# A masked mixing product, VectorE cycles with four tiles, and a first tile by column halves, in an fp8 and 4-bit feed-forward kernel

## The chip, the cores and the metric

The kernel runs on 1 core of one Trainium2 chip. The metric is the device time of one execution in microseconds, the median of several runs. The kernel before takes 527.69 us (three runs, 527.61 to 528.54). The traces are of one profiled execution each; its span begins with the first and ends with the last instruction.

## What is computed

x is 64 samples x 64 channels x 1024, float32. Cut to what matters:

```python
# 1: a mixture of K = 8 channel-mixing matrices, weighted per sample
att = softmax(mlp(cond))                                   # (64, 8), three layers, exact gelu
m   = einsum('boi,bih->boh', einsum('bk,koi->boi', att, weight), x) + (att @ bias_k)[:, :, None]
# 2: a linear layer in fp8 (e4m3), with ONE scale for all of m and one for the weight
xs, ws = max|m| / 448, max|W0| / 448
x1  = x + fp8(m / xs) @ fp8(W0.T / ws) * (xs * ws) + b0
# 3: a grouped convolution along the 1024 positions (64 channels, 4 groups, 9 taps) plus a per-sample
#    term, then a linear layer with 4-bit weights (groups of 128, a scale and a zero for each)
y   = conv(x1) + (c @ c_weight.T)[:, :, None] + side
out = x1 + y @ ((W1_q - zero) * scale).T + b1
```

The scale in step 2 needs the largest |m| of all 64 samples. So no tile can be quantised before every tile has been mixed and reduced.

## The kernel before

**Tiles.** Two samples of 64 channels make a tile of 128 partitions x 1024; there are T = 32. All mixed tiles stay in the buffer Y (`slot(t)`, 32 slots of 128 x 1024). Slots also hold other things until a tile is loaded there: slots 16 to 20 the 4-bit weight's row blocks 0 to 4 (`w1i(n)`), slot 21 and 22 the taps, slot 23 the small network, slots 24 to 31 the eight row slices of W0 (`w0f`).

**The opening** (lines 446 to 563, 744 to 794, 1016 to 1058). TensorE runs the three-layer network. The mixing weights, 8 x 64 x 64, are split on VectorE into three bf16 parts (`wk_parts`), and nine DMAs gather the parts into `wkp9`. The attention weights get the same split and are transposed; 32 products give the mixing matrices, which ACT and VectorE (`place_last`) copy into `mixw`, a block-diagonal 128 x 128 matrix for each tile. VectorE also takes the largest |W0| of each slice as it lands (`largest_w0`, L758). The maximum of all 128 partitions is found by a transpose and a product with ones on TensorE (`w_pe`): the exchange. Then comes the weight's scale (`scales`).

**The cycles** (lines 840 to 850). Then VectorE runs eight cycles, r = 0 to 7: round slice r of W0 to the fp8 grid (L730, L733, L735), subtract the zeros of block r of W1 (`less_w1`, L820), and reduce mixed tiles (`largest_mixed`, L805: tiles 3r+1 and 3r+2 in one instruction, then 3r+3). `groups` lists these as (first tile, tiles); an entry waits until ACT has kept its last tile. What is left of the tiles follows behind cycle 7. POOL ends the rounding (`round_w0`, L490) and multiplies W1 with its scales (`times_w1`, L484).

**TensorE and ACT** walk the tiles in order, t = 0 to 31. TensorE mixes tile t in two halves (`mixed_tile`, L1064); behind tile 3r+6 it turns slice r of W0 (`turned0`, waits for POOL's rounding), behind tile 3n+8 block n of W1 (`turned1`, waits for POOL's product; both L1080). ACT keeps tile t with its bias (L582), copies the turned blocks to `f0T` and `f1T` (L589), and behind tile 3r-1 scales slice r (`scale_w0`, L601), which for r >= 2 waits for POOL's rounding of slice r-2, whose buffer it uses again.

**SP's queue** issues loads in program order, each behind its wait. Tiles 16 to 20 wait for `less_w1` of the block whose slot they take, tiles 24 to 31 for POOL's rounding of the slice.

**The exchange of the mixed maximum, and the first tiles** (lines 851 to 968, 1214 to 1245). When the last reduction is done, TensorE transposes the maxima (L1220) between sums over the turned W1 (`weight_sums`, L1198). Then `scales`, and the first tiles: widen (L864, L868), mask the bits (L873), quantise (L882, L887), turn, multiply with W0 (`first_ffn0`, L1154), add the residual (`residual0`, L912), split x1 into two fp16 parts (`hi` on ACT L642, `lo` on VectorE L922), move the parts to the convolution's layout by eight DMAs per tile (`move`, L412 on SP and L533 on POOL), and convolve (`conv`, L1180). `keep_clock` and `keep_clock_wide` are products whose result is used nowhere.

**The steady part.** From tile 2 on, for every tile TensorE runs 16 products with W0, 32 with W1 and 48 for the convolution; the other engines and the queues work beside it.

Of the kernel before, what the change touches and what calls it, by code (L numbers as in the profile page):

```python
# [5 lines left out]
def adaln_ffn_kernel(nc, x, cond, fside, cw0, cb0, cw1, cb1, cw2, cb2, cwk, cbk,  # L6
# [21 lines left out]
    P = 128  # L28
# [23 lines left out]
    with ctx:  # L52
# [29 lines left out]
        def mix_src(m, par, b):  # L82

            return pair[m][par * C:(par + 1) * C, :].rearrange("p (j t b) -> p b t j", t=T, b=NB)[:, b]

        def mix_dst(m, par, b):
            o = b * C + 32 * m + par
            return mixw[b * C:(b + 1) * C, :, o:o + 31:2]
# [11 lines left out]

        def w1c(n):
# [12 lines left out]
        wkf, wkr = (work[0:K * KC, 5 * L + n * KF:5 * L + (n + 1) * KF] for n in range(2))  # L114
        wkp = work[0:K * KC, 6 * L:6 * L + 3 * KF // 2].bitcast(bf16).rearrange("p (e f) -> p e f", e=3)
        attp9 = slot(19)[0:B, 0:36].bitcast(bf16)
        attp = attp9.rearrange("p (k i e) -> p i e k", i=3, e=3)
        attr = slot(19)[0:B, 40:40 + K]
        attpT = slot(19)[0:KP, 64:64 + B // 2].bitcast(bf16)
# [12 lines left out]
        att = mlp[0:B, 840:848]  # L132
        attT = mlp[0:K, 848:912]
# [5 lines left out]
        mbk2 = f0T[0:K, R8 - 1, 0:2 * P].bitcast(fp32)  # L139
# [13 lines left out]
        o += R8 * SW  # L153
        convin = work[:, o:o + BG * SW].bitcast(fp16).rearrange("p (g s e) -> p g s e", g=BG, e=2)
# [50 lines left out]
        ld = {n: sem("ld_" + n) for n in ("emb", "mw0", "mw1", "mw2", "ctw", "mbk", "wk", "wkp", "wkl", "fcol", "zs", "b0", "b1",  # L205
# [16 lines left out]
        wk_parts = sem("wk_parts")  # L222
# [4 lines left out]
        att_parts = sem("att_parts")  # L227
        attp_mm = sem("attp_mm")
        attp_ev = sem("attp_ev")
# [62 lines left out]
        turns0 = {3 * r + 6: r for r in range(R8)}  # L292
        turns1 = {3 * n + 8: n for n in range(KT)}
        turn_order = []
        for t in range(T):
            if t in turns0:
                turn_order.append(("w0", turns0[t]))
            if t in turns1:
                turn_order.append(("w1", turns1[t]))

# [15 lines left out]
        def _(sp):  # L316
# [21 lines left out]
            load_w0(3)  # L338
            load_w0(4)
            for b in range(NB):  # L340
                sp.dma_start(mbk2[:, b * C:(b + 1) * C], cbk).then_inc(ld["mbk"], 16)
            load_w0(5)
            load_mixing(0)
# [4 lines left out]
            for n in range(7):  # L348
                for t in range(2 * n + 1, 2 * n + 3):
                    load_mixing(t)  # L350
                if n == 3:
                    sp.wait_ge(mix_mm, 2)
                load_w1(n)
# [4 lines left out]
            load_mixing(15)  # L358
            for t in range(16, 21):
# [4 lines left out]
            sp.wait_ge(taps_split, 4)  # L364
            load_mixing(21)
            load_mixing(22)
# [3 lines left out]
            for r in range(R8):  # L370
# [3 lines left out]
                load_mixing(W0_SLOT + r)  # L374

# [40 lines left out]
            sp.wait_ge(moved_sp[1], 32)  # L416
# [29 lines left out]
        def _(pool):  # L446
# [847 lines left out]
```

## Time and profile before

| | |
|---|---|
| median of 3 runs | 527.69 us |
| profiled execution | 527.88 us |
| its span | 526.1 us |
| TensorE busy | 511.2 us, 97% |
| VectorE busy | 414.4 us, 79% |
| ACT busy | 243.9 us, 46% |
| POOL busy | 59.3 us, 11% |

In the rows, PE is TensorE, PEld its weight loads, DVE is VectorE, ACT ScalarE, POOL GpSimd, SP SyncE; a q behind a name is the engine's own DMA queue. A line number is that of the kernel before. "out<-in" names the buffers: Y holds the tiles, work and fixed are scratch, pair is PSUM. Times are microseconds from the start of the span. In brackets stands the idle time ahead of an instruction and what ended it.

### The profile page before, as it was taken

The numbers are of one execution on the slowest core, as the hardware profiler recorded it, in microseconds if no ns is written. First come the engines' busy times: TensorE is split into PE (matmuls) and PEld (weight loads), VectorE is DVE, ScalarE is ACT, GpSimd is POOL, SyncE is SP. The second block draws the span as 40 slices with busy tenths as digits, with TensorE's granted clock in tenths as the row PEclk, the third lists the DMA queues.
The fourth block names the chain that finished last, engine by engine and source line by source line (L and its number), as shares of the span: only waits on it lengthen the run. The fifth ranks groups of instructions, "written<-read, shape, count | busy, mean of one in ns | idle before, by whom it ended". The sixth has DMA issues, their size and how long they took to land.

```text
span 526.1 us, 9556 instructions
## 1 busy us (share of the span) xinstructions
PE 511.2 (97%) x3528; PEld 286.0 (54%) x3528; DVE 414.4 (79%) x526; ACT 243.9 (46%) x286; POOL 59.3 (11%) x68
## 2 busy tenths in 40 slices
PE   5799999999999999999999999999999999999997
PEld 4544444355555555555555555555555555555564
DVE  6899999877887777777777777777777777777652
ACT  3479897754344444444444444444444444442310
POOL 5276666020000000000000000000000000000000
PEclk9999999999999999999999999999999999999999
DMA  7999681235675655566666565555566656565632
GB/s 225 393 386 405 222 329 42 80 82 142 185 218 182 181 181 181 181 181 181 181 181 181 181 181 181 181 181 181 182 183 182 182 183 180 183 185 186 199 122 80
DMA packets 85795, 100.61 MB, mean 191 GB/s; under 512 B 34484, under 2 KB 67318, under 8 KB 85782
## 3 DMA queue, kind: packets, MB, share of 16 engines
q1 hardware_dynamic: 84754, 99.41, 59.2%
q0 software_dynamic: 656, 0.82, 0.9%
q10 hardware_dynamic: 372, 0.20, 0.1%
q8 instruction: 8, 0.13, 0.1%
q14 instruction: 5, 0.04, 0.0%
HBM read 58.41 MB, written 32.75 MB: 173 GB/s over the span
## 4 chain that ended last, share of the span: by engine, by line
PE 81%; DVE 11%; issue 2%; DMA 2%; SPq 1%; ACT 1%; POOL 1%; DVEq 0%; ACTq 0%; POOLq 0%
PE pair L1190 41%; PE pair L1164 19%; PE pair L1180 16%; DVE stat L805 5%; DMA Y<-in_L_ffn_weight_dram 2%; PE pair L1154 1%; PE pair L1064 1%; DVE work L730 1%; DVE work L820 1%; DVE Y L820 1%; DVE work L733 1%; PE pair L1267 1%; SPq L337 1%; POOL fixed L490 1%; DVE work L742 1%
## 5 line engine op out<-in xcount | busy, mean ns | idle before, releaser
L1190 PE MATMUL pair<-f1T,work 128*128 128x512 f16 x1008 | 227.5, 379 | 0.0
L1190 PEld LDWEIGHTS pair<-f1T,work 128*128 128x128 f16 x1008 | 97.2, 98 | 111.7 <-DVE work L929 0.2
L609 ACT ACTIVATE work<-Y,consts 128x1024 bf16 (+1 forms) x29 | 33.3, 1149 | 185.7 <-DVE work L903 185.7
L922 DVE TENSOR_TENSOR work<-Y,work 128x512 f16<-128x512 f16 (+1 forms) x64 | 71.2, 1120 | 47.2 <-ACT work L642 46.3
L1164 PE MATMUL pair<-f0T,work 128*128 128x512 bf16 x464 | 104.9, 379 | 0.0
L1180 PEld LDWEIGHTS pair<-taps,work 128*128 128x128 f16 x1536 | 88.3, 98 | 8.0 <-issue 0.5
L1180 PE MATMUL pair<-taps,work 128*128 128x128 f16 x1536 | 91.0, 219 | 0.0
L642 ACT CAST work<-Y 128x512 f16 (+1 forms) x64 | 69.5, 1136 | 18.6 <-DVE Y L912 15.6
L935 DVE TENSOR_TENSOR Y<-pair,Y 128x512 f32 (+1 forms) x63 | 43.3, 687 | 41.3 <-PE pair L1190 41.3
L1164 PEld LDWEIGHTS pair<-f0T,work 128*128 128x128 bf16 x464 | 45.3, 98 | 54.8
L1064 PE MATMUL pair<-Y,work 128*128 128x512 f32 x128 | 60.6, 608 | 0.4 <-ACT Y L582 0.4
L647 ACT CAST work<-pair 128x512 f16<-128x512 f32 x64 | 37.1, 585 | 33.4 <-PE pair L1180 31.9
L941 DVE SCALAR_TENSOR_TENSOR pair<-work,consts,fixed 128x512 f32<-128x512 f32 x63 | 47.3, 753 | 0.1
L912 DVE SCALAR_TENSOR_TENSOR Y<-pair,stat,Y 128x512 f32 (+1 forms) x64 | 45.0, 743 | 1.2 <-PE pair L1164 1.2
L929 DVE TENSOR_TENSOR work<-pair,work 128x512 f16<-128x512 f32 x64 | 41.2, 683 | 2.5 <-ACT work L647 2.5
L582 ACT ACTIVATE Y<-pair,consts 128x1024 f32<-128x1024 f32 (+1 forms) x33 | 35.9, 1092 | 12.4 <-PE pair L1064 12.3
L896 DVE SCALAR_TENSOR_TENSOR Y<-work,Y 128x1024 bf16 (+1 forms) x29 | 35.5, 1225 | 4.0
L805 DVE TENSOR_REDUCE stat<-Y 128x1 f32<-128x1024 f32 (+2 forms) x23 | 36.4, 1629 | 0.7 <-ACT Y L582 0.6
L903 DVE SCALAR_TENSOR_TENSOR work<-work,Y 128x1024 bf16<-128x1024 bf16 x29 | 35.5, 1225 | 1.2
L1064 PEld LDWEIGHTS pair<-Y,work 128*128 128x128 f32 x128 | 22.8, 194 | 22.0 <-issue 20.4
L610 ACT ACTIVATE Y<-Y,stat (+1 forms) x29 | 32.9, 1134 | 0.0
L490 POOL TENSOR_TENSOR fixed<-Y,work 128x1024 bf16<-128x1024 f32 x8 | 24.0, 3004 | 18.6 <-DVE Y L735 18.6
(161 smaller groups left out, 251.5 us busy)
## 6 DMA issues: line engine op xcount, KB each, us to landing
Y<-in_x_dram SPq DMA_DIRECT2D x64, 512.0 KB, 3.9
out_dram<-Y SPq DMA_DIRECT2D x31, 512.0 KB, 3.7
split_rows<-work SPq DMA_DIRECT2D x30, 520.0 KB, 2.6
work<-split_rows SPq DMA_DIRECT2D x30, 520.0 KB, 3.9
Y<-in_L_ffn_weight_dram SPq DMA_DIRECT2D x8, 512.0 KB, 7.3
Y<-in_L_ffn_W_q_dram SPq DMA_DIRECT2D x5, 512.0 KB, 14.2
work<-in_L_ffn_W_q_dram SPq DMA_DIRECT2D x3, 512.0 KB, 15.2
work<-work SPq DMA_DIRECT2D x8, 65.0 KB, 3.7
```

The costliest lines, as they stand in the source:

```text
L642: nc.scalar.copy(split[:, r, h:h + S, 0], v[:, r, :]).then_inc(hi_done, 1)
L647: nc.scalar.copy(y1s[n][:, 0, :, b * C:(b + 1) * C].rearrange("p r (g a) -> p g r a", g=G), ps[4 + b][:, :].rearrange("p (g r a) -> p g r ...
L805: nc.vector.tensor_reduce(stat[:, n:n + 1], part, AX.X, ALU.max, apply_absolute_value=True).then_inc(mixed_red, 1)
L912: nc.vector.scalar_tensor_tensor(out=v, in0=ps[h][:, :], scalar=acc_neg, in1=v, op0=ALU.mult, op1=ALU.add).then_inc(x1_done, 1)
L922: nc.vector.tensor_tensor(split[:, r, s, 1], v[:, r, :], split[:, r, s, 0], ALU.subtract)\
L929: nc.vector.tensor_tensor(part(1), ps[4 + b][:, :].rearrange("p (g r a) -> p g r a", g=G, r=R8), part(0), ALU.subtract).then_inc(ylo_done, 1)
L935: nc.vector.tensor_tensor(v, ps[2 + h][:, :], v, ALU.add).then_inc(res_done, 1)
L941: nc.vector.scalar_tensor_tensor(out=ps[2 + h][:, :], in0=wsum[:, c], scalar=ctxcol[:, bass.ds(t, 1)], in1=fixed[:, c], op0=ALU.mult, op1= ...
L1064: last = mm(ps[2 * (t % 2) + h][:, :], mixw[:, t, :], slot(t)[:, h * H:(h + 1) * H], start=True, stop=True)
L1164: last = mm(ps[h][:, :], qT[n][:, k, :], f0T[:, k, h * H:(h + 1) * H], start=(k == 0), stop=(k == KT - 1))
L1180: last = mm(ps[4 + b][:, g * P:(g + 1) * P], convin[:, b * G + g, h:h + S, xp], taps16[:, wp, h, g].rearrange("p r a -> p (r a)"), start=( ...
L1190: last = mm(ps[2 + h][:, :], y1s[n][:, e, k, :], f1T[:, k, h * H:(h + 1) * H], start=False, stop=(e == 1 and k == KT - 1), skip_group_chec ...
```

## The change

**Mixing matrices.** The three-part split and its gathers go. `wkf` becomes 128 rows (8 matrices x 16 groups of 4 output channels) of 256; the attention weights, repeated 16 times, are transposed and multiplied with a mask `own_c` (the columns of an identity summed), which gives `attM`, 128 x 16 x 64. Four fp32 products of 512 columns give the mixing matrices. The first load of `wkf` moves from ACT's queue to POOL's.

**Order.** Two slices of W0 are reduced ahead of `place_last`, six behind it. Tiles 0 to 2 are reduced within the exchange of the weight's maximum, whose transpose stands behind tile 3 on TensorE and whose product stands within tile 4. The cycles take four tiles each (0 to 4), then three. The turns stand at other tiles, the last three behind all tiles. The last tile is loaded to scratch and is not blocked by slice 7.

**First tiles.** The first product runs by column halves, its residual, split and low part too. Ten of the idle products near the first convolution become six.

The diff, cut to its core:

```diff
-        KP = 9 * K
-        wkp9 = Y[0:KP, 20 * L:22 * L].bitcast(bf16)
-        KC = C // K
+        KC = P // K
         KF = C * C // KC
+        KR = K * KC
+        wkf = work[0:KR, 5 * L:5 * L + KF]
+        attM = work[0:KR, 6 * L:6 * L + KC * B].rearrange("p (c b) -> p c b", c=KC)
...
-        groups = [(0, 1)] + [g for r in range(R8) for g in ((3 * r + 1, 2), (3 * r + 3, 1))]
-        groups += [(25, 2), (27, 2), (29, 1), (30, 1), (31, 1)]
-        groups[-1:] = [(31, 0), (31, 1)]
+        beside = [[(0, 1), (1, 1)], [(2, 1)]]
+        cycle_groups = [[(3, 2), (5, 2)], [(7, 2), (9, 2)], [(11, 2), (13, 2)], [(15, 2), (17, 2)], [(19, 2), (21, 2)],
+                        [(23, 2), (25, 1)], [(26, 2), (28, 1)], [(29, 2), (31, 0), (31, 1)]]
...
-        turns0 = {3 * r + 6: r for r in range(R8)}
-        turns1 = {3 * n + 8: n for n in range(KT)}
+        turns0 = {3 * r + 9 if r < R8 - 1 else T - 1: r for r in range(R8)}
+        turns1 = {3 * n + 10: n for n in range(KT - 2)}
...
@@ sync
-            for e in range(2):
-                sp.wait_ge(wk_parts, (1, 3)[e])
-                for i in range(3):
-                    sp.dma_start(wkp9[3 * i + e:KP:9, :], wkp[:, e, :]).then_inc(ld["wkp"], 16)
             load_w0(3)
+            load_mixing(0)
+            sp.wait_ge(mbk_zero, 1)
...
             load_mixing(15)
+            sp.wait_ge(taps_split, 4)
+            load_mixing(21)
+            load_mixing(22)
             for t in range(16, 21):
                 sp.wait_ge(w1_less, t - 15)
                 load_mixing(t)
             sp.wait_ge(wT_mm, turn_at("w1", 1) + 1)
             load_w1(7)
-            sp.wait_ge(taps_split, 4)
-            load_mixing(21)
-            load_mixing(22)
...
-            for r in range(R8):
+            for r in range(R8 - 1):
                 sp.wait_ge(w0q, r + 1)
                 if r < 2:
                     sp.wait_ge(wT_mm, turn_at("w1", 3 + r) + 1)
                 load_mixing(W0_SLOT + r)
+            for h in range(2):
+                sp.wait_ge(w1_less, 6 + h)
+                sp.dma_start(last_raw(h), x_t[T - 1, :, h * H:(h + 1) * H]).then_inc(ld_x[T - 1], 16)
...
@@ scalar
+                    if t == T - 1:
+                        act.wait_ge(w0q, R8)
                     nc.scalar.activation(slot(t)[:, c], pair[t % 2][:, c], ACT.Identity, bias=aggcol[:, t:t + 1])\
...
-                if t == 2:
+                if t == 5:
                     act.wait_ge(w_step, 2)
-                if t % 3 == 2 and t <= 20:
-                    scale_w0(t // 3 + 1)
+                if t % 3 == 2 and 5 <= t <= 23:
+                    scale_w0(t // 3)
...
+            for n in (KT - 2, KT - 1):
+                keep_w1(n)
             keep_sums(0)
...
             first_scaled(2)
+            act.wait_ge(pads, 3)
+            first_hi(0)
             for h in range(2):
                 keep_first_q(1, h)
-            act.wait_ge(pads, 3)
-            hi(0)
+            first_hi(1)
...
@@ vector
-            for r in range(1, 5):
-                largest_w0(r)
-            place_last()
-            for r in range(5, R8):
+            largest_w0(0)
+            largest_w0(1)
...
+            place_last()
+            for r in range(2, R8):
                 largest_w0(r)
             dve.wait_ge(w_red, R8)
             nc.vector.tensor_reduce(w_part, w_rows, AX.X, ALU.max).then_inc(w_red, 1)
+            largest_mixed(0)
+            largest_mixed(1)
             dve.wait_ge(w_pe, 1)
             nc.vector.tensor_reduce(w_all, ps[7][0:1, 0:P], AX.X, ALU.max).then_inc(w_red, 1)
+            largest_mixed(2)
             dve.wait_ge(w_pe, 2)
...
                 less_w1(r)
-                if r == 0:
-                    largest_mixed(0)
-                largest_mixed(2 * r + 1)
-                largest_mixed(2 * r + 2)
-            for n in range(2 * R8 + 1, NGRP):
-                largest_mixed(n)
+                for g in cycle_groups[r]:
+                    largest_mixed(groups.index(g))
...
             first_widen(1)
-            first_quantise(1)
+            first_quantise(1, (0,))
             dve.wait_ge(x_step, 4)
-            residual0(0, 0, 16)
+            residual0(0, 0, 16, (0,))
+            first_quantise(1, (1,))
+            residual0(0, 0, 16, (1,))
+            first_lo(0)
+            first_lo(1)
             first_widen(2)
-            lo(0)
...
@@ tensor
+            pe.wait_ge(idle_zero, 1)
+            keep_clock(5, H)
...
-            for q in range(4):
-                for j in range(8):
-                    o2 = 8 * q + j
-                    last = mm(ps[q][:, j * B:(j + 1) * B], wkp9[:, o2 * 2 * C:(o2 + 1) * 2 * C],
-                              attpT, start=True, stop=True)
-                if q % 2:
-                    last.then_inc(mix_mm, 1)
+            for h in range(2):
+                pe.wait_ge(mlp_ev, 8 + h)
+                for m in range(2):
+                    last = mm(ps[2 * h + m][:, :], wkf[:, m * 2 * C:(m + 1) * 2 * C],
+                              attM[:, h * KC // 2:(h + 1) * KC // 2].rearrange("p c b -> p (c b)"),
+                              start=True, stop=True)
+                last.then_inc(mix_mm, 1)
...
-                if t == 0:
+                if t == 3:
                     pe.wait_ge(w_red, R8 + 1)
                     nc.tensor.transpose(ps[7][0:1, 0:P], w_part, ident[:, :]).then_inc(w_pe, 1)
...
-            pe.wait_ge(wT_ev, 2 * KT)
+            for n in (KT - 2, KT - 1):
+                turned1(n)
+            pe.wait_ge(wT_ev, 2 * KT - 2)
...
+            pe.wait_ge(wT_ev, 2 * KT)
             weight_sums(1, range(KT))
...
-            first_ffn0(0, 0, 0)
+            first_ffn0_by_columns()
...
-            keep_clock_wide(10)
+            keep_clock_wide(6)
```

## Rows read from the trace of the kernel before

**Rows 1.** The page: busy engines, and TensorE's clock in 40 slices.
```profile
PE 511.2 (97%) x3528; PEld 286.0 (54%) x3528; DVE 414.4 (79%) x526; ACT 243.9 (46%) x286; POOL 59.3 (11%) x68
...
PEclk9999999999999999999999999999999999999999
```

**Rows 2.** Chain that ended last: start us, us, engine, tile, line, how many.
```profile
30.18 4.45 DVE stat L805 x3
...
115.39 3.45 PE pair L1154 x16
```

**Rows 3.** A stage: window and length, busy us (how many) by engine, clock, DMA share, GB/s.
```profile
15.00:45.00 30.00, 28.61 (x140) 15.87 (x141) 27.61 (x32) 21.18 (x26) 15.97 (x12) 1.00 1.03 396
```

**Rows 4.** Timeline of cycle 1: start us, us, engine, line, operation, out<-in.
```profile
34.54 0.42 DVE L730 TENSOR_SCALAR work<-work 128x1024 int16<-128x1024 int16 x1
...
36.66 1.22 DVE L820 TENSOR_TENSOR work<-Y,small 128x1024 f16<-128x1024 int32 x1
36.83 3.05 POOL L490 TENSOR_TENSOR fixed<-Y,work 128x1024 bf16<-128x1024 f32 x1 [1.10 <-DVE Y L735]
...
37.80 3.41 DVE L805 TENSOR_REDUCE stat<-Y 128x1 f32<-128x2048 f32 x2
...
41.12 0.91 DVE L730 TENSOR_SCALAR work<-work 128x1024 int16<-128x1024 int16 x1
```

**Rows 5.** Timeline around the turn of the last slice of W0.
```profile
76.22 3.65 PE L1064 MATMUL pair<-Y,work 128*128 128x512 f32 x8
...
78.19 1.11 ACT L582 ACTIVATE Y<-pair,consts 128x1024 f32<-128x1024 f32 x1 [0.20 <-PE pair L1064]
...
79.71 0.65 PE L1080 MATMUL pair<-small,work 128*128 128x128 f16 x8
...
82.35 0.62 PE L1080 MATMUL pair<-small,fixed 128*128 128x128 bf16 x8 [0.22 <-POOL fixed L490]
...
85.93 3.41 DVE L805 TENSOR_REDUCE stat<-Y 128x1 f32<-128x2048 f32 x2
```

**Rows 6.** SP's queue: the load of tile 20, and its time to landing (line 321).
```profile
59.12 0.34 SPq L321 DMA_DIRECT2D Y<-in_x_dram  x1
...
DMA to landing us min/median/max: 3.2/3.2/3.2
```

**Rows 7.** Groups of 0 to 115 us: busy us, mean ns | idle before.
```profile
L589 ACT COPY f0T<-pair 128x1024 bf16<-128x1024 bf16 x8 | 8.1, 1012 | 0.0
...
L484 POOL TENSOR_TENSOR work<-work,small 128x1024 f16<-128x1024 f16 x5 | 9.6, 1911 | 0.0
...
L601 ACT ACTIVATE work<-Y,stat 128x1024 bf16<-128x1024 f32 x7 | 8.0, 1138 | 0.0
```

**Rows 8.** Timeline of the opening.
```profile
8.40 1.89 PE L1014 MATMUL pair<-small 128*128 128x128 bf16 x16
...
15.11 1.89 PE L1047 MATMUL pair<-Y 72*128 72x64 bf16 x32 [1.70 <-DMA Y<-work]
...
20.34 2.55 PE L1064 MATMUL pair<-Y,work 128*128 128x512 f32 x4
...
22.71 1.22 DVE L758 TENSOR_REDUCE stat<-Y 128x1 f32<-128x1024 f32 x1 [0.17 <-DMA Y<-in_L_ffn_weight_dram]
...
26.84 0.43 DVE L730 TENSOR_SCALAR work<-work 128x1024 int16<-128x1024 int16 x1
```

**Rows 9.** Timeline of the exchange of the mixed maximum.
```profile
89.91 2.41 DVE L805 TENSOR_REDUCE stat<-Y 128x1 f32<-128x1024 f32 x3 [0.56 <-ACT Y L582]
...
92.58 0.27 PE L1220 MATMUL pair<-ident,stat 128*1 128x128 f32 x1 [0.96 <-DVE stat L852]
...
94.33 0.88 DVE L864 TENSOR_SCALAR work<-Y,stat 128x512 bf16<-128x512 f32 x2
```

**Rows 10.** Timeline of the first tiles.
```profile
104.99 2.12 DVE L922 TENSOR_TENSOR work<-Y,work 128x512 f16<-128x512 f32 x2 [0.19 <-ACT work L642]
...
112.54 2.85 PE L1180 MATMUL pair<-taps,work 128*128 128x128 f16 x48
```

More of the change, by code:

```diff
@@ L107, in adaln_ffn_kernel @@
         mixw = work[:, 0:T * P].rearrange("p (t m) -> p t m", t=T)
-        KP = 9 * K
-        wkp9 = Y[0:KP, 20 * L:22 * L].bitcast(bf16)
-        KC = C // K
+        KC = P // K
         KF = C * C // KC
[L114 to L119, printed above, removed]
+        KR = K * KC
+        wkf = work[0:KR, 5 * L:5 * L + KF]
+        attM = work[0:KR, 6 * L:6 * L + KC * B].rearrange("p (c b) -> p c b", c=KC)
+        idle_rows = f1T[:, 0, 0:H]
         wide_taps = f0T[:, 0, 0:CG * R8 * 4].bitcast(fp32).rearrange("p (c j) -> p c j", c=CG)
@@ L642, in hi, with first_hi @@
                     nc.scalar.copy(split[:, r, h:h + S, 0], v[:, r, :]).then_inc(hi_done, 1)
+            def first_hi(h):
+                act.wait_ge(x1_done, h + 1)
+                s = slice(h * S // 2, (h + 1) * S // 2)
+                v = slot(0).rearrange("p (s u r) -> p u r s", u=2, r=R8 // 2)
+                nc.scalar.copy(skewed[:, :, :, s, 0], v[:, :, :, s]).then_inc(hi_done, 1)
             def yhi(t, n):
@@ L913, in residual0, with first_lo @@
                                                    op1=ALU.add).then_inc(x1_done, 1)
+            def first_lo(h):
+                dve.wait_ge(hi_done, h + 1)
+                s = slice(h * S // 2, (h + 1) * S // 2)
+                v = slot(0).rearrange("p (s u r) -> p u r s", u=2, r=R8 // 2)
+                nc.vector.tensor_tensor(skewed[:, :, :, s, 1], v[:, :, :, s], skewed[:, :, :, s, 0], ALU.subtract)\
+                    .then_inc(lo_done, 1)
             def lo(t):
@@ L1055, in _, with turned_tap_rows @@
-            last.then_inc(taps_mm, 1)
+            nc.tensor.transpose(ps[6][0:KR, 256:256 + B], attR, ident[0:B, 0:B]).then_inc(mlp_mm, 1)
+            def turned_tap_rows(ws):
+                pe.wait_ge(taps_made, 3)
+                for w in ws:
+                    last = nc.tensor.transpose(pair[2][:, w * P:(w + 1) * P],
+                                               taps_rows[:, w].rearrange("p c r -> p (c r)"), ident[:, :])
+                if w == R8 - 1:
+                    last.then_inc(taps_mm, 1)
@@ L1063, in mixed_tile @@
                 for h in range(2):
-                    last = mm(ps[2 * (t % 2) + h][:, :], mixw[:, t, :], slot(t)[:, h * H:(h + 1) * H],
-                              start=True, stop=True)
+                    raw = last_raw(h) if t == T - 1 else slot(t)[:, h * H:(h + 1) * H]
+                    last = mm(ps[2 * (t % 2) + h][:, :], mixw[:, t, :], raw, start=True, stop=True)
                     if h or t == T - 1:
                         last.then_inc(mixed, 1)
-                    if t == 1 and h == 0:
+                    if t == 4 and h == 0:
                         pe.wait_ge(w_red, R8 + 2)
@@ L1142, in keep_clock_wide, with first_ffn0_by_columns @@
                     mm(ps[5][:, :], ident_b, f0T[:, 0, 0:H], start=True, stop=True)
+            def first_ffn0_by_columns():
+                for h in range(2):
+                    pe.wait_ge(shifted_ev, h + 1)
+                    for k in range(KT):
+                        if h == 0 and k % 4 == 0:
+                            pe.wait_ge(qT_in[0], 2 * k + 8)
+                        last = mm(ps[h][:, :], qT[0][:, k, :], f0T[:, k, h * H:(h + 1) * H],
+                                  start=(k == 0), stop=(k == KT - 1))
+                    last.then_inc(f0_done, 1)
             def first_ffn0(t, n, before):
```

178 lines of the change are left out of this document (82 added, 96 removed).

## The prediction, made before the changed kernel ran

> **What bounds the kernel now.** I read the page first: a span of 526.1 us, TensorE busy 97% of it [rows 1]. Then the chain of work that ended last, which falls into two parts: up to about 92 us it runs mostly on VectorE, through the reductions that look for the largest mixed value; from 115.39 us on it is TensorE without a break [rows 2]. The change touches nothing there. So its worth is how much earlier or later that part starts. I call S the start of the first widening (line 864), which needs the scale of all mixed tiles: 94.33 us now [rows 9].
>
> **The VectorE cycles.** Before S, VectorE runs eight cycles, one for each slice r of the first weight. I call C_r the start of line 730 in cycle r; C_0 is 26.84 [rows 8]. Counted from C_r = 34.54: the rounding is done and `less_w1` starts at +2.12, ends at +3.34, the reductions start at +3.26 (starts overlap ends a little), and the next cycle starts at +6.58 [rows 4]. So a pair of tiles and a single one together take 3.32. In the first cycle two singles and a pair take 4.45 [rows 2]: a single 1.12, a pair 2.20. The last three, a single and two halves, take 2.41 [rows 9]: a half 0.66. Line 730 takes 0.42 when POOL is idle and 0.91 when POOL's product of the cycle before still runs, as in most cycles now [rows 4]. POOL rounds slice r until C_r + 5.34 (36.83 + 3.05 [rows 4]); its product of 1.91 follows [rows 7].
>
> **The change, part by part.**
>
> *Opening.* The split weights, their gather DMAs and three bf16 parts go; four fp32 products on a masked operand replace them. Now the first mixed tile starts at 20.34, 5.2 us behind the 32 products that wait for the gather until 15.11 [rows 8]. The four new products need no gather; at half a tile's time each (0.87, as two tiles take 3.49 from 76.22 to 79.71 [rows 5]) and with the same copies behind them they allow the first tile at about 17 to 18. That isn't what starts the cycles. That is the eight reductions of the weight. Two now stand ahead of `place_last` and six behind it: if it is done at 17, six times 1.15 lead to 23.9, as now (22.71 + 1.22 [rows 8]), although the last slice, whose load waits no longer for the split, should land 2 to 3 us earlier. Then come the reductions of three tiles, put into the exchange of the weight's scale (3.4 us), and the exchange itself, now 2.9 from 23.93 to 26.84 [rows 8], of which they fill about 1.0. Sum: 23.9 + 3.4 + 1.9 = 29.2 for C_0, 2.4 later, with three tiles done. The exchange stands behind tiles 3 and 4 on TensorE, whose loads arrive at 396 GB/s, 1.3 us each [rows 3]; that leaves C_0 between 28 and 30.5.
>
> *Work in the cycles.* Cycles 0 to 4 reduce four tiles: 3.26 + 2 x 2.20 = 7.66, and POOL is through (5.34 + 1.91 = 7.25, with its issue 7.4) just before the next line 730, so that this is taken at 0.42. Cycles 5 and 6: 6.58 each. Cycle 7: 3.26 + 2.20 + 1.32 = 6.78. Sum 58.2. With no wait VectorE would be through at 29.2 + 58.2 = 87.4, against 92.32 now [rows 9].
>
> *Waits in the cycles.* The turns of the weight move three tiles back (slice r behind tile 3r + 9), the loads of tiles 16 to 20 stay behind `less_w1`, and the reductions move forward: cycle r wants tiles up to 4r + 6. These cross. From rows: 1.97 after TensorE starts a tile (76.22), ACT starts to keep it (78.19) and takes 1.11, so VectorE has it 3.1 after the start; a tile behind a turn that waited for POOL until 82.3 is reduced from 85.93, 3.6 later [rows 5]. ACT takes 1.01 for a turn, 1.14 for `scale_w0` [rows 7].
> Cycle 2: ACT's own load, with turns and scales beside the tiles, gives tile 14 between 0 and 2.1 late; I take 1.0.
> Cycle 3 wants tile 18. ACT must first do `scale_w0(5)`, which waits for POOL's round 3 (+5.34); then 1.14 + 1.12 and issue: +7.7 against +5.46. **2.2**.
> Cycle 4 wants tiles 19 and 20 at +3.26, but tile 20's slot is the source of `less_w1(4)`, so its load is issued only when that ends, at +3.34. Now the same load is issued at 59.12, right behind its `less_w1`, (SP's queue had waited for it), and lands 3.2 later [rows 6], but is reduced two cycles later. Landed +6.6, free for VectorE +9.7: **6.4**. Behind it stands the load of the last W1 piece, then tiles 23 to 25; they arrive in time.
> Then tile 22: ACT has `scale_w0(6)`, tile 21, the turn of slice 4 and tile 22, 4.4 us, while VectorE has 2.20 of work: **2.2**.
> Cycle 5 wants tile 24: ACT stands at `scale_w0(7)` for round 5: +7.7 against +3.26: **4.4**. Tile 25 follows in time.
> Cycle 6 wants tile 28, which TensorE mixes behind turn 6: 5.34 + 3.6 = +9.0 against +5.46: **3.5**.
> Cycle 7: tile 31 is kept after round 7: **0.6**.
> Sum 20.3; VectorE is through at 107.7. None of these waits exists now; the one wait shown for a tile is 0.56, before the last reductions [rows 9].
>
> *From the last reduction to S.* Now 2.0 us, 92.32 to 94.33 [rows 9]. After it TensorE stands behind three turns in order; the last needs ACT to have kept slice 7 (C_7 + 7.8), then 0.5, then five sums (1.15) and the transpose at C_7 + 9.5, instead of at 7.5. With the 1.75 from the transpose (92.58) to line 864 [rows 9] S is C_7 + 11.3, 3.9 after the last reduction: 111.6.
>
> *First tile by column halves.* Its first product half ends 0.7 earlier, but the second half of the split waits for the second residual, which is behind one more quantisation: the low part is written by S + 12.3 instead of 12.8 (104.99 + 2.12 [rows 10]). The moves to the convolution start 0.5 earlier. Widening of tile 2 falls behind it, so the last turn of tile 2 is 0.65 later, but ten filler products become six, 0.9 less at 0.22 each (16 of 512 columns in 3.45 [rows 2]). The convolution starts at S + 18.0 instead of 18.2 [rows 10]: 0.2 gained. Bounds: 0.8 gained, if the fillers are all that counts, and 0.8 lost, if the last turn of tile 2 is. Clearing, the early idle products and the constants moved on POOL and ACT lie under the reductions of the weight, which end where they did; without that cover I put them at 1 us at most, inside C_0's bounds. The DMAs of the window and of b0 stay on POOL and end before their use, as far as the turns allow: b0 behind the last turn (C_7 + 8.4, then 2 to 3), its user at C_7 + 12.8.
>
> *TensorE's speed.* In cycle 4 TensorE would stand still for about 7 us, from the turn of W1 slice 3 to tile 20, in 5 and 6 for about 5. The trace has no such stretch once it is at speed. But the first filler products, 128 columns wide, come every 0.105 us (16 in 1.89 [rows 8]), and the same shape later every 0.056 (8 in 0.62 [rows 5]; each sum holds one product's full 0.2 to 0.3), and the first mixed tile takes 2.55, where two now take 3.65 [rows 8, 5]. That is the level of 1.2 GHz in the beginning, behind idling, and of 2.4 later, though the page's clock row reads 9 throughout [rows 1]. I take one fall, in the longest stretch: tile 20 costs 1.74 more. The Trainium skill (TensorE: Matmul & The Clock Gate, section Why this matters for your kernels) warns that idle gaps between bursts of matmuls bring the slow clock back; by that all three stretches would count, which is rival (a).
>
> **Sum.** S: 29.2 + 58.2 + 20.3 + 3.9 = 111.6, that is 17.3 later; less 0.2, plus 1.7 for the clock: 18.8. The profiled execution took 527.88 (526.1 in the span, 1.8 around it), 0.2 above the median of 527.69: 546.5 on the scale of the runs.
>
> **The rivals.**
> (a) The clock falls in all three stretches. Cycle 5 then costs 1.2 more (ACT hides the rest), cycle 6 2.2: 549.9. For it: the slow rows at the start. Against: these stretches are shorter, and ACT and VectorE may hide more. 0.25.
> (b) The clock never falls: 544.8. For it: the page's clock row never leaves 9 [rows 1], so it may be something else that is slow in the beginning. 0.20.
> (c) Only tile 20's load holds VectorE, and what waits there is caught up elsewhere, because the other tiles stand ready by then: waits of 8.6 instead of 20.3, no further clock cost: about 533 (546.5 less 11.7 and less the 1.7). Against: `scale_w0` and the turns stand in fixed order on ACT and TensorE. 0.06.
> (d) Faster. VectorE's work alone decides: it would be so if tile 20 were mixed before C_4 + 3.26 and the tiles behind the turns likewise. Then the last reduction ends at 87.4 instead of 92.32, S is 91.3, and the kernel takes 524.5. For it: VectorE is nearly without idle time now, and POOL no longer slows line 730. Against: the load of tile 20 can't be issued before `less_w1(4)` ends. 0.03.
> The forecast has 0.46.
>
> **Range and chances.** From (b) with the opening 1 us better and no wait in cycle 2 (542.8) to (a) with the opening 1.3 worse and 1 more in cycle 2 (552.2): 542 to 552. It leaves out (c), (d) and the tails of the others. A measurement can tell 0.2% (1 us) from no change; slower by more 0.96, faster by more 0.03, within 0.01.
>
> **What the profile will show.** VectorE's idle time ahead of the mixed reductions grows from 0.6 to about 20 us, released by ACT, with one wait of over 6 us behind `less_w1(4)`; ACT waits for POOL ahead of `scale_w0`; TensorE has one gap near 7 us and two near 5; line 730 mostly takes 0.42; S is near 112, and from the first convolution on all is as now. A first cycle at 26 or a mixed tile 20 within C_4 + 4 would make this wrong.

## The result and the profile after

The changed kernel takes 554.6 us (median of 4 runs, 553.76 to 555.52), the kernel before beside it 527.84. The ratio is 1.050, 95% interval 1.048 to 1.053. The forecast was 546.5, with a range of 542 to 552: the direction was right, the loss was 8 us larger than I said. The profiled execution took 555.52 (span 553.5), 27.6 more than the one of before.

From the page of the changed kernel:

```profile
span 553.5 us, 9438 instructions
PE 521.7 (94%) x3460; PEld 288.3 (52%) x3492; DVE 411.2 (74%) x519; ACT 244.7 (44%) x284; POOL 58.1 (10%) x67
...
PEclk9999987798999999999999999999999999999999
```

The clock row now dips in slices 6 to 8 and 10, where that of before has none [rows 1]. VectorE's instructions in the cycles (start, duration, engine, line; in brackets the idle time ahead and who ended it):

```profile
28.81 0.43 DVE L741 TENSOR_SCALAR work<-work 128x1024 int16<-128x1024 int16 x1
...
51.48 2.29 DVE L809 TENSOR_REDUCE stat<-Y 128x1 f32<-128x2048 f32 x1 [1.53 <-ACT Y L583]
...
61.22 2.29 DVE L809 TENSOR_REDUCE stat<-Y 128x1 f32<-128x2048 f32 x1 [2.01 <-ACT Y L583]
63.42 0.42 DVE L741 TENSOR_SCALAR work<-work 128x1024 int16<-128x1024 int16 x1
75.02 2.29 DVE L809 TENSOR_REDUCE stat<-Y 128x1 f32<-128x2048 f32 x1 [8.27 <-ACT Y L583]
79.27 2.29 DVE L809 TENSOR_REDUCE stat<-Y 128x1 f32<-128x2048 f32 x1 [1.96 <-ACT Y L583]
81.47 0.42 DVE L741 TENSOR_SCALAR work<-work 128x1024 int16<-128x1024 int16 x1
89.00 2.29 DVE L809 TENSOR_REDUCE stat<-Y 128x1 f32<-128x2048 f32 x1 [4.19 <-ACT Y L583]
92.60 1.22 DVE L809 TENSOR_REDUCE stat<-Y 128x1 f32<-128x1024 f32 x1 [1.32 <-ACT Y L583]
...
104.86 1.22 DVE L809 TENSOR_REDUCE stat<-Y 128x1 f32<-128x1024 f32 x1 [5.60 <-ACT Y L583]
...
112.13 1.28 DVE L809 TENSOR_REDUCE stat<-Y 128x1 f32<-128x512 f32 x2 [0.60 <-ACT Y L583]
```

L741 is the first line of a cycle (L730 before), so C_0 is 28.81 and C_4 63.42; L809 is the reduction of mixed tiles. Its waits add up to 25.7 us in nine places; before there was one, of 0.56 [rows 9]. TensorE's rows show where the tiles come from, again with the idle time in brackets:

```profile
70.06 5.80 PE L1081 MATMUL pair<-Y,work 128*128 128x512 f32 x8 [6.98 <-DMA Y<-in_x_dram]
...
86.88 1.01 PE L1096 MATMUL pair<-small,fixed 128*128 128x128 bf16 x8 [4.81 <-issue]
...
99.15 1.01 PE L1096 MATMUL pair<-small,fixed 128*128 128x128 bf16 x8 [3.71 <-issue]
```

The gap of 6.98 ends with the load of tile 20; those of 4.81 and 3.71 stand ahead of the turns of W0 slices 5 and 6, which wait for POOL's rounding. Behind each gap TensorE is slow: eight mixing products take 5.80, where they took 3.65 [rows 5], and a turn 1.01 instead of 0.62. The stretches with TensorE's busy time and count, and then, third from the end, the granted clock:

```profile
64.00:67.00 3.00, 0.00 (x0) 0.00 (x0) 2.72 (x3) 0.64 (x1) 1.24 (x1) 1.00 0.00 0
68.00:74.00 6.00, 3.94 (x5) 1.85 (x6) 0.00 (x0) 0.12 (x1) 2.60 (x2) 0.50 0.89 335
82.00:84.00 2.00, 0.07 (x1) 0.00 (x0) 1.96 (x3) 0.00 (x0) 0.19 (x1) 1.00 1.03 420
86.00:90.00 4.00, 3.12 (x11) 1.95 (x12) 1.00 (x1) 3.05 (x3) 2.65 (x2) 0.50 0.39 131
96.00:98.00 2.00, 0.00 (x0) 0.00 (x0) 2.00 (x2) 0.59 (x1) 1.92 (x1) 1.00 0.00 0
100.00:104.00 4.00, 4.00 (x7) 1.74 (x6) 0.00 (x0) 1.30 (x2) 0.92 (x1) 0.50 0.79 262
119.00:121.00 2.00, 0.14 (x1) 0.18 (x2) 1.97 (x5) 1.95 (x3) 0.92 (x5) 1.00 0.03 4
123.00:128.00 5.00, 4.78 (x13) 1.58 (x13) 1.57 (x4) 3.24 (x6) 0.00 (x0) 0.50 0.30 105
```

0.50 is the level of 1.2 GHz, 1.00 that of 2.4. There are four such stretches of just under 7 us: three begin while TensorE stands still in one of the gaps (at 67.5, 84.6 and 98.2) and last into the work behind it; the fourth begins at 122.1, behind S, which none of my cases had. S is the start of L867, 117.28, 23.0 later than before. What follows it on TensorE:

```profile
116.78 1.90 PE L1224 MATMUL pair<-f1T,consts 128*27 128x512 f16 x8
120.86 1.09 PE L1232 MATMUL pair<-work 29*128 29x512 f32 x2 [2.17 <-issue]
121.88 0.43 PE L1152 MATMUL pair<-small,work 128*128 128x128 bf16 x4
122.24 2.07 PE L1237 MATMUL pair<-work 29*128 29x512 f32 x2
124.24 0.61 PE L1152 MATMUL pair<-small,work 128*128 128x128 bf16 x4
125.07 5.32 PE L1166 MATMUL pair<-f0T,work 128*128 128x512 bf16 x15 [0.22 <-issue]
...
139.50 1.67 PE L1206 MATMUL pair<-taps,work 128*128 128x128 f16 x27
```

L1232 is `fixed_part(0)`; it waits 2.17 us for the rows of b0 and b1 (the two biases, loaded by small DMAs on POOL's queue). Then L1237 takes 2.07 for what L1232 did in 1.09. The first convolution (L1206) starts at S + 22.2, where it was S + 18.2 [rows 9, 10]. POOL's rows tell why b0 and b1 are late:

```profile
111.28 1.90 POOL L489 TENSOR_TENSOR work<-work,small 128x1024 f16<-128x1024 f16 x1
113.14 0.20 POOL L513 CAST consts<-consts 128x16 f16<-128x16 f32 x1
113.42 0.23 POOL L515 TENSOR_TENSOR consts<-consts 128x16 f16<-128x16 f32 x1
113.63 0.54 POOL L518 DMA_DIRECT2D work<-in_L_ffn_bias_dram  x1
117.60 1.06 POOL L522 CAST fixed<-work 1x1024 f32<-1x1024 f16 x1 [3.43 <-DMA work<-in_L_ffn_bias_dram]
118.61 0.63 POOL L524 DMA_DIRECT2D work<-in_L_ffn_bias_dram  x1
119.24 0.48 POOL L526 DMA_DIRECT2D work<-fixed  x1
```

The load of b1's row stands in POOL's program behind the last product, which ends at 113.18, 4 us ahead of S. The cast waits 3.43 for it, and the two DMAs that `fixed_part` needs are issued only after the cast.

### The profile page after: what moved, and what is told of

Same layout as the page of the kernel before. It is cut to its first block, busy times and chain, and to the rows that moved or that the text cites. A ratio compares the mean times of both kernels' runs of the same rounds, so it can differ in the third digit from the quotient of the medians.

```text
span 553.5 us, 9438 instructions
## 1 busy us (share of the span) xinstructions
PE 521.7 (94%) x3460; PEld 288.3 (52%) x3492; DVE 411.2 (74%) x519; ACT 244.7 (44%) x284; POOL 58.1 (10%) x67
## 4 chain that ended last, share of the span: by engine, by line
PE 81%; DMA 4%; SPq 4%; issue 4%; DVE 3%; ACT 2%; POOL 1%; DVEq 0%; ACTq 0%; POOLq 0%
PE pair L1216 38%; PE pair L1190 18%; PE pair L1206 15%; PE pair L1081 5%; DMA Y<-in_x_dram 3%; ACT Y L583 1%; POOL fixed L495 1%; DVE stat L809 1%; DMA work<-work 1%; PE pair L1096 1%; SPq L325 1%; PE pair L1166 1%; PE pair L1224 1%; SPq L328 1%; SPq L331 1%
## 5 line engine op out<-in xcount | busy, mean ns | idle before, releaser
L933 DVE TENSOR_TENSOR work<-Y,work 128x512 f16<-128x512 f16 (+1 forms) x62 | 69.1, 1120 | 45.1 <-ACT work L643 43.9
L1190 PE MATMUL pair<-f0T,work 128*128 128x512 bf16 x435 | 98.6, 379 | 2.1 <-DMA work<-work 0.7
L1206 PEld LDWEIGHTS pair<-taps,work 128*128 128x128 f16 x1536 | 88.4, 98 | 7.7 <-issue 0.4
L1206 PE MATMUL pair<-taps,work 128*128 128x128 f16 x1536 | 91.0, 219 | 0.0
L643 ACT CAST work<-Y 128x512 f16 (+1 forms) x62 | 67.5, 1138 | 16.6 <-DVE Y L915 15.6
L1081 PE MATMUL pair<-Y,work 128*128 128x512 f32 x124 | 64.5, 660 | 9.3 <-DMA Y<-in_x_dram 8.1
L809 DVE TENSOR_REDUCE stat<-Y 128x1 f32<-128x2048 f32 (+2 forms) x20 | 36.9, 1854 | 25.7 <-ACT Y L583 25.7
L1081 PEld LDWEIGHTS pair<-Y,work 128*128 128x128 f32 x124 | 24.1, 210 | 35.4 <-issue 23.0
```

Source lines behind the costliest of these rows:

```text
L643: nc.scalar.copy(split[:, r, h:h + S, 0], v[:, r, :]).then_inc(hi_done, 1)
L809: nc.vector.tensor_reduce(stat[:, n:n + 1], part, AX.X, ALU.max, apply_absolute_value=True).then_inc(mixed_red, 1)
L933: nc.vector.tensor_tensor(split[:, r, s, 1], v[:, r, :], split[:, r, s, 0], ALU.subtract)\
L1081: last = mm(ps[2 * (t % 2) + h][:, :], mixw[:, t, :], raw, start=True, stop=True)
L1190: last = mm(ps[h][:, :], qT[n][:, k, :], f0T[:, k, h * H:(h + 1) * H], start=(k == 0), stop=(k == KT - 1))
L1206: last = mm(ps[4 + b][:, g * P:(g + 1) * P], convin[:, b * G + g, h:h + S, xp], taps16[:, wp, h, g].rearrange("p r a -> p (r a)"), start=( ...
```

## The experiments

My theory: the reductions were moved forward and the loads, scalings and turns that feed them were not, so VectorE waits; the slow clock is a consequence. The rivals: the opening, the first tile, the clock by itself. In each run the kernel before ran on the same chip; its median lay between 527.4 and 528.9.

### Three reductions a cycle, in the changed kernel

```diff
-        cycle_groups = [[(3, 2), (5, 2)], [(7, 2), (9, 2)], [(11, 2), (13, 2)], [(15, 2), (17, 2)], [(19, 2), (21, 2)],
-                        [(23, 2), (25, 1)], [(26, 2), (28, 1)], [(29, 2), (31, 0), (31, 1)]]
+        cycle_groups = [[(3 * r + 3, 2), (3 * r + 5, 1)] for r in range(R8)]
+        cycle_groups[-1] += [(27, 2), (29, 2), (31, 0), (31, 1)]
```

> The changed kernel, with its reductions of the mixed tiles put back to three a cycle (tile 3r + 3, 3r + 4 as a pair, 3r + 5 alone; the rest behind the last cycle). Opening, turns and first tile stay as changed. My theory: the order of the reductions is what costs, because four a cycle ask for tiles that the loads and turns, left behind, don't give yet. Then the 25.7 us of VectorE waits go down to under 2, no stretch of TensorE's slow clock is left before S, S falls from 117.3 to 92 to 94, and the kernel takes 527 to 532 (the late row of b1 may still cost up to 3 of it). Rival, the opening costs it: 545 or more. Rival, the first tile by column halves costs it: S falls as above, but the kernel stays 4 us or more behind its S.

527.86 us, ratio 1.0011 (0.9986 to 1.0035). VectorE waits for no mixed tile any more. Two waits are left, one in the exchange of the weight's maximum, ahead of the first cycle (L841), and one in that of the mixed maximum, behind the last reduction (L857):

```profile
engine line waited for: us in total, times, longest us
DVE stat L841 <- PE pair L1114: 0.9, 1, 0.9
DVE stat L857 <- PE pair L1248: 0.4, 1, 0.4
```

C_0 is 28.47 (the opening is late as forecast), S 92.29, the convolution at 110.75. The whole loss is gone with this one edit. So neither the opening nor the first tile costs it alone.

### What the opening gives alone

The same with the first tile as before.

```diff
-            first_ffn0_by_columns()
+            first_ffn0(0, 0, 0)
...
-            keep_clock_wide(6)
+            keep_clock_wide(10)
```

(and the residual, quantisation and split of tile 0 in the old order)

> The changed kernel with three reductions a cycle and the first tile as before: only the new opening is left of the change. My theory: the opening starts the first cycle 1.6 us later, but with three tiles already reduced the last reduction ends 2 us earlier than before: S 92 to 92.6, and the kernel 1 to 2 us faster than before (0.2 to 0.4%). Rival, what is gained up to S is lost behind it: no difference from the kernel before.

528.83, ratio 1.0003 (0.9978 to 1.0028): no difference, as the rival said. In its profiled execution S was 94.51, not 92 to 92.6: TensorE waited 3.17 for the load of a tile and the clock fell behind that, too. Executions differ here by as much as the opening could give: with the new one and three a cycle S was 91.5, 92.3 and 94.5 in three kernels, with the one of before 92.7, 93.6 and 94.3. That the opening gains anything is not shown.

### One subtraction a cycle earlier

```diff
-                less_w1(r)
+                if r != 4:
+                    less_w1(r)
+                if r == 3:
+                    less_w1(4)
```

> The changed kernel, with one W1 slice's subtraction (number 4, whose source is the slot of tile 20) done one cycle earlier, so that tile 20's load is issued a cycle earlier. My theory: the load was worth 6.4 us plus 1.7 for the slow clock behind it, but what waits next (turns and scales, 2 us in that cycle, more in the next) is shared, so 5 to 8 us go: 546.5 to 549.5. Rival, the wait is only moved to the scale and turn of the next slice: under 2 us go.

547.82, 6.8 less. The gap of 6.98 is gone and no slow clock is left there, but VectorE still waits 4.12 in cycle 4, now for the turn of slice 4, and 4.19, 0.73 and 5.60 in cycles 5 and 6, nearly as in the changed kernel. The load was one of several waits, as forecast.

### Everything moved along

```diff
-        turns0 = {3 * r + 9 if r < R8 - 1 else T - 1: r for r in range(R8)}
-        turns1 = {3 * n + 10: n for n in range(KT - 2)}
+        turns0 = {t: r for r, t in enumerate((9, 12, 15, 18, 22, 25, 28, 31))}
+        turns1 = {t: n for n, t in enumerate((10, 13, 16, 19, 22, 26))}
+        scales_at = {t: r + 1 for r, t in enumerate((5, 9, 13, 17, 21, 24, 27))}
```

with the subtraction above; ACT now scales at the tiles of `scales_at`.

> The changed kernel with four reductions a cycle kept, and what was left behind moved along with them: W1 slice 4's subtraction a cycle earlier (as in the run before), the scalings of the weight slices on ACT behind tiles 5, 9, 13, 17, 21, 24, 27, the turns of W0 behind tiles 9, 12, 15, 18, 22, 25, 28, 31, those of W1 behind 10, 13, 16, 19, 22, 26. My theory: the waits come from the order of these instructions against the reductions, nothing else. VectorE's waits fall from 25.7 to 5 to 7 us, TensorE has no gap over 3 us and no slow clock before S, S is 97 to 101, and the kernel takes 531 to 537. Rival, the work itself (loads, ACT's time) doesn't allow four a cycle: waits stay above 12 us and the time above 541.

535.69. The waits of VectorE over the cycles:

```profile
DVE stat L810 <- ACT Y L584: 5.4, 7, 1.5
```

5.4 instead of 25.7, the longest 1.5; S is 97.43, and no slow clock ahead of it (one fall, behind S). The instructions are the same; only the place of some of them in their queues has changed. That shows the theory. Even so the kernel is 1.6% slower than before (1.2 to 2.0%), and S is 5.1 later than with three a cycle. So four a cycle gains nothing in this order; whether an order without the last waits would, is not shown.

### Idle products in the gaps

`fill(n)` is n products of 128 columns whose result is used nowhere.

```diff
+                if t == 20:
+                    pe.wait_ge(tapsum_made, 1)
+                    fill(90)
                 mixed_tile(t)
+                if t == 24:
+                    fill(60)
+                if t == 27:
+                    fill(45)
```

> The changed kernel, with idle products on TensorE in its three long gaps (90 of 128 columns ahead of tile 20, 60 behind tile 24, 45 behind tile 27), so that it never stands still there. They compute nothing that is used. My theory: the slow clock in the three stretches is a consequence of these gaps and costs about 1.9, 1.3 and 2.1 us in them: the granted clock stays at 1.00 up to S, the VectorE waits fall from 25.7 to 20 to 21 (my forecast's sum), and the kernel takes 548 to 551. Rival, the clock is the main cost: it falls under 540. Rival, the slow clock is hidden beside ACT and VectorE: under 2 us go.

551.67, 2.9 less, so just outside what I expected. Gaps of 2.12, 1.99 and 2.50 us were left, and the granted clock still fell to 0.50 behind them, 0.6, 0.6 and 2.6 us after their ends (ahead of the last fall stood one more gap, of 1.18); not behind one of 1.47. It fell a fourth time behind S, 1.3 us after a gap of 2.58. VectorE waited 23.0. So the same with more of them (125 ahead of tile 20, then 85, 80, 45 and 20 twice):

> The changed kernel with more idle products than in the first such run (125 ahead of tile 20, 85 behind tile 24, 80 behind 27, 45 behind 31, 20 behind each of the last two turns), so that no gap of TensorE before S is over about 1.3 us. In the run with fewer of them gaps of 2.0 to 2.5 us were left, and the granted clock still fell to 0.50 right behind three of them (but not behind one of 1.5). My theory: without such gaps the clock stays at 1.00 up to S, VectorE waits 20 to 21 us, S is 111 to 113 and the kernel takes 547.5 to 550. Rival, the falls don't come from standing still (the amount of work or something outside decides): as many falls as before, waits at 23 or more, 551 or more.

548.54. The only gap of over 1.3 us that was left is ahead of tile 20, and the only fall ahead of the convolution is behind it (clock column third from the end):

```profile
69.00:71.00 2.00, 0.05 (x1) 0.00 (x0) 0.00 (x0) 0.00 (x0) 1.10 (x1) 1.00 0.92 354
72.00:74.00 2.00, 2.00 (x4) 0.71 (x3) 0.00 (x0) 0.00 (x0) 0.00 (x0) 0.50 0.60 240
82.00:84.00 2.00, 2.00 (x27) 1.43 (x26) 1.93 (x4) 0.30 (x1) 0.00 (x0) 1.00 0.96 332
86.00:90.00 4.00, 3.89 (x43) 2.74 (x41) 0.17 (x1) 2.35 (x3) 3.49 (x2) 1.00 0.48 172
...
100.00:104.00 4.00, 4.00 (x11) 1.70 (x10) 1.81 (x3) 2.47 (x3) 0.36 (x1) 1.00 0.68 240
```

VectorE's waits, with the clock up from cycle 5 on:

```profile
76.14 2.29 DVE L809 TENSOR_REDUCE stat<-Y 128x1 f32<-128x2048 f32 x1 [9.89 <-ACT Y L583]
80.10 2.29 DVE L809 TENSOR_REDUCE stat<-Y 128x1 f32<-128x2048 f32 x1 [1.67 <-ACT Y L583]
89.83 3.41 DVE L809 TENSOR_REDUCE stat<-Y 128x1 f32<-128x2048 f32 x2 [4.20 <-ACT Y L583]
102.16 1.22 DVE L809 TENSOR_REDUCE stat<-Y 128x1 f32<-128x1024 f32 x1 [3.46 <-ACT Y L583]
109.44 1.28 DVE L809 TENSOR_REDUCE stat<-Y 128x1 f32<-128x512 f32 x2 [0.61 <-ACT Y L583]
```

Cycles 5, 6 and 7 wait 4.20, 3.46 and 0.61, where I had put 4.4, 3.5 and 0.6 without the clock. Cycle 4 waits more than in the changed kernel, because tile 20's mixing began 5.0 us after its load was issued (3.3 there). With that, and the idle products behind the turns, which delayed the exchange by 1.1, the sum of waits (22.9) and S (115.7) were outside what I expected, though the time was within. So ahead of S the slow clock comes from TensorE standing still. The run took 6.1 us less than the changed kernel, but not all of that is the clock of the three gaps: of the 6.3 between the profiled executions 1.6 lie ahead of S (117.28 to 115.70), 3.9 between S and the convolution (S + 22.2 to S + 18.3) and 0.7 behind it. The 3.9 are the fourth fall, which is gone, and b1's row: S now comes 5.2 us after the end of POOL's last product instead of 4.1, and `fixed_part(0)` waits 0.31 instead of 2.17. So the time was within my range partly by luck. The clock alone can't explain the loss: with it held in cycles 5 to 7, 22.9 us of waits stay.

### b1's row earlier

First on POOL, ahead of its last product:

```diff
                 round_w0(r)
+                if r == R8 - 1:
+                    pool.wait_ge(w1_less, KT)
+                    pool.dma_start(b1_row, f1b.rearrange("(a n) -> a n", a=1)).then_inc(ld["b1"], 16)
                 times_w1(r)
```

(and the same DMA gone from its old place)

> The changed kernel, with the DMA of the row of b1 issued from POOL ahead of its last product instead of behind it. My theory: b1's row and b0 behind it hold fixed_part(0) for 2.2 us, and TensorE's slow clock right behind costs about 2 more: 550 to 552. Rival, the stretch behind S is slow anyway (the slow clock comes from the thin work ahead of S): only the 2.2 go, 552 to 553. Rival, it is fully covered: no change from 554.6.

553.76, 0.8 less, above both ranges that I had given for a gain; their intervals against the kernel before (1.048 to 1.053 and 1.043 to 1.052) overlap, so it can't be told from no change. `fixed_part(0)` waited no more and the convolution started at S + 18.9, but S itself was 1.8 later, 1.4 of it between the last reduction and S (5.2 instead of 3.8): the DMA's issue, 0.54 on POOL, pushed back the last product and with it the last turn, and this and the sums behind it ran at the slow clock (turn 1.07 instead of 0.69, five sums 2.15 instead of 1.25). A step was moved past one that others waited for, which is the fault of the change in small. So once more from SP's queue, which is idle there:

```diff
+            sp.wait_ge(w1_less, KT)
+            sp.dma_start(b1_row, row(f1b)).then_inc(ld["b1"], 16)
```

> The changed kernel, with the row of b1 loaded by SP's queue behind the last W1 subtraction, so that POOL's last product isn't put off by it (in the run with POOL's DMA moved it was 0.5 us later, and S 1.8 later). My theory: late b1 and b0 cost 2.2 us behind S: fixed_part(0) follows the weight sums without a gap (at S + 1.3, not S + 3.6), the first convolution starts at S + 18.5 if the clock holds behind S and up to S + 20.5 if it falls; 550.5 to 552.5. Rival, the first tile is held by something else (the load of x for the residual, the slow clock): the convolution stays at S + 22 and the time at 554 or more.

552.2, 2.4 less. POOL's cast has no wait (the row was issued at 107.60), and `fixed_part(0)` starts at S + 1.3:

```profile
111.66 0.23 POOL L517 TENSOR_TENSOR consts<-consts 128x16 f16<-128x16 f32 x1
111.83 1.03 POOL L522 CAST fixed<-work 1x1024 f32<-1x1024 f16 x1
112.93 0.54 POOL L524 DMA_DIRECT2D work<-in_L_ffn_bias_dram  x1
```

The convolution starts at S + 19.0, with the clock at 0.50 from 120.1 to 123.5 all the same. The same edit in the kernel with everything moved along:

> The run with four a cycle and everything moved along (535.7 us), with b1's row loaded by SP's queue as well. My theory: fixed_part(0) waited 1.8 us for it there and the clock fell once behind S; without both the convolution starts at S + 18.5 instead of S + 20.6: 532.5 to 534.5. Rival, covered by the load of x for the residual: no change, 535.7.

532.77, 2.9 less; clock 1.00 throughout, convolution at S + 18.2. It is still 0.75% above the kernel before (0.3 to 1.2%). The last run of this kind has both edits, three a cycle and b1's row early on POOL, in the changed kernel:

> Three reductions a cycle and b1's row early, together. My theory: what is left of the change (opening, first tile) is worth between nothing and 2 us: 526 to 529, S between 92 and 94. Rival, the opening and the first tile cost on their own: over 530.

529.1, just above the 526 to 529 that I expected, ratio 1.0014 (0.9987 to 1.004), S 91.5: against the run with three a cycle alone (1.0011) no gain from the row is to be seen. In its profiled execution the clock fell once, behind S (96.0 to 99.4), and the convolution started at S + 19.2.

### The first tile alone

The kernel before with the change's first tile (column halves, six fillers).

> The kernel before, with the change's part on the first tile alone (split and product by column halves, six fillers instead of ten). My theory: 0.3 us faster to 0.5 slower; the first convolution starts at S + 17.8 to S + 18.6, where it is S + 18.2 now. Rival, this part is what makes the first tile 4 us longer in the changed kernel: 2 us or more slower.

527.38, ratio 0.9984 (0.9967 to 1.0001). The convolution starts at S + 18.5, as in the run with three a cycle. The row that I had not foreseen:

```profile
100.25 0.75 DVE L921 SCALAR_TENSOR_TENSOR Y<-pair,stat,Y 128x512 f32<-128x512 f32 x1 [0.77 <-DMA Y<-in_x_dram]
```

The first residual now stands ahead of tile 1's second quantised half, and the load of x for it has only just landed; TensorE's turn of that half waits 1.26. In the first run with idle products the same residual waited 2.10 and the turn 2.58. So, with both quantised halves ahead of the residual:

```diff
             first_quantise(1, (0,))
+            first_quantise(1, (1,))
             dve.wait_ge(x_step, 4)
             residual0(0, 0, 16, (0,))
-            first_quantise(1, (1,))
```

> The kernel before with the first tile by column halves, but both halves of tile 1's quantisation ahead of both residual halves of tile 0. With the change's order VectorE waited 0.8 us for the load of x ahead of the first residual, and TensorE 1.3 us for the second quantised half. My theory: both waits go, the last turn of tile 1 comes at S + 8, and the convolution starts at S + 17.6 to 18.2: 0.3 to 0.8 us faster than with the change's order (527.4), which is near what can be told. Rival, the moves of the split rows, now later by a residual, set the convolution's start: no difference, or 0.5 slower.

527.51, ratio 0.9973 (0.9952 to 0.9995). The turn waits no more, but the product of tile 1 now waits 0.82 for ACT and the convolution starts at S + 18.7: the miss of my theory, no difference to the run before. Both are by their ratios 0.2 and 0.3% faster than the kernel before, the second with an interval that ends 0.05% short of no change; nothing that I tried is clearly better than that.

## Why the prediction was short

Forecast 18.8 us later, measured 27.6 between the profiled executions. The step that failed most is the first tile, put at 0.2 us gained where 4.0 were lost; the second is the slow clock, put at one fall of 1.7 where three cost 5.3 ahead of S. Step by step (a plus or minus is a difference to the kernel before, the others are lengths in the changed kernel):

| step | forecast | measured |
|---|---|---|
| C_0 | +2.4 | +2.0 (28.81 against 26.84) |
| VectorE's work in the cycles | 58.2 | 58.9 (113.44, where the last maximum starts, less C_0 and the waits) |
| waits in the cycles, without the clock | 20.3 | 20.4 (25.7 less the 5.3 of the next line) |
| slow clock ahead of S | 1.7 | 5.3 |
| last reduction to S | 3.9 | 3.8 |
| first tile to the convolution | -0.2 | +4.0 |
| behind it | 0 | +0.7 |

C_0, work, waits with the clock, and the exchange make S: 28.8 + 58.9 + 25.7 + 3.8 = 117.2.

- **The order's waits were right**, one by one: forecast 1.0, 2.2, 6.4 + 2.2, 4.4, 3.5, 0.6 for cycles 2 to 7; measured 1.53, 2.01, 8.27 + 1.96, 4.19 + 1.32, 5.60, 0.60. What is above it is 1.87 in cycle 4, 1.32 in cycle 5 and 2.10 in cycle 6. That these are the clock's is shown for cycles 5 and 6 by the run with more idle products, which has no second wait in cycle 5 and 3.46 instead of 5.60 in cycle 6. In cycle 4 the fall could not be taken away; there VectorE has tile 20 4.96 us after TensorE starts it (70.06 to 75.02), where the rows at full clock give 3.1 [rows 5].
- **The clock step failed in its count, not in its price.** I took one fall, in the longest gap. It fell behind all three, which was rival (a), with prices of 1.7, 1.2 and 2.2 for them. I had argued that gaps of 5 us were shorter and might be hidden; here the clock fell in gaps of 4.81 and 3.71, and in other runs behind some of about 2. The rule of the Trainium skill that I had beside it (TensorE: Matmul & The Clock Gate, section Why this matters for your kernels) was the better guide: idle gaps between bursts of matmuls did bring the slow clock back, here behind gaps of 4.81 and 3.71 us as behind the one of 6.98. The clock row on the profile's page of before, at 9 throughout, had been no argument for (b), as that trace has no gap over 1.7 us once TensorE has begun. Nor does the granted clock bear out what I read from the opening: it is 1.00 in the opening of both kernels, although sixteen products of 128 columns take 1.89 us there and twenty take 1.28 later; why is open.
- **The first tile failed as a term**: -0.2 against +4.0, outside its bounds of 0.8. I wrote that the DMAs of b0 end before their use, b0 behind the last turn and 2 to 3 us long, its user at C_7 + 12.8. That left out the chain on POOL ahead of it: b1's load, waited for 3.43, then the cast of 1.06, then b0's two DMAs. `fixed_part(0)` starts at C_7 + 14.9. In the kernel before the same chain, with a wait of 1.97 in it, had its last DMA issued by 89.3, 5.0 ahead of S; now that is 2.4 behind S, and nothing hides it. The run from SP's queue takes it away: the convolution comes 3.2 earlier after S, of which 2.2 are the wait, and for the rest the slow stretch behind S is 3.4 us long instead of just under 7. What is left, S + 19.0 against 18.2, is the fall: with the column halves and at most 0.3 of waiting for b1 the convolution starts at S + 18.9 to 19.2 in the three executions in which the clock fell at the first product, and at S + 18.2 to 18.5 in four in which it didn't. What the load of x adds is too small to be told from this; in the changed kernel the first residual waits for TensorE (3.80), not for it. I had followed only the last link of it.
- **C_0, the exchange and the end** came within 0.7 us of what was worked out. Rival (c), waits that are caught up elsewhere, and rival (d), VectorE's work alone, are out: with tile 20's load moved, 16.8 us of waits stay.

Rival (a)'s 549.9 with the first tile's 4.2, and 0.7 behind the convolution, comes to 554.8, against 554.6.

## What to carry over

When the consumer of a pipeline is moved forward, list for each item that it wants what stands ahead of that item in every in-order queue (loads, scalings, turns), because these stay where they were; here taking the consumer back to its old place gave all of the loss back, and moving the others along took 20 of the 26 us of waits away. Price every long gap that this opens on TensorE with a fall of its clock, not only the longest (here all of 3.17 us and more had one), and take gaps of 2 to 3 us as a chance, for they went either way. And where the end of a stage comes nearer to a background engine's last work, follow that engine's whole chain of small DMAs to its user: it was hidden only by distance.

## What the runs showed of the hardware

- The granted clock fell to 0.50 in or right behind every gap of TensorE of 3.17 us or more in these traces (twelve, up to 7.37). Between 1.9 and 2.8 us it did either: it fell within 2.6 us behind 1.99, 2.12, 2.17, 2.22, 2.50 and twice 2.58, and not behind 1.92, 1.95, 2.19, 2.41 (everything moved along, with b1's row), 2.44 and 2.71 (three a cycle, with and without b1's row), nor behind 1.47 and 1.83. Behind S it fell after 1.69 and 1.77, too. So length alone doesn't decide there.
- It also fell, for about 3.4 us, behind S where TensorE's only gap in the 5 us just ahead was one of 0.4 us (b1's row earlier on POOL and from SP's queue, three a cycle with b1's row early, and three a cycle with the first tile of before), while the run with three a cycle alone, with nearly the same rows, kept it at 1.00. What decides there is open.
- Idle products of 128 columns held the clock at 1.00 in stretches of 4.6 to 7.1 us in which TensorE had nothing else to do; what stands behind them starts later if there are too many. 125 of them took 7.14 us.
- A load of 512 KB took from its issue to its first use 3.2 to 5.0 us at the same place in the program, with other loads queued behind it.
- The first line of a cycle takes 0.42 where POOL's product of the cycle before is through; with four reductions a cycle it did so in all eight cycles.
